# One core, two attention layers: the key-maxima matmuls of the graph layer get a new placement and order on TensorE

## The reference, cut to what matters

```
for c in range(6):                        # nodes; sources are earlier nodes
    q = ew[c, 0] * (nodes[in_q] @ We[eq] + be[eq])
    k = ew[c, 1] * (nodes[in_k] @ We[ek] + be[ek])
    v = ew[c, 2] * (nodes[in_v] @ We[ev] + be[ev])
    o = _mha(q, k, v, Wq[c], Wk[c], Wv[c], Wo[c])     # 8 heads of 16, softmax over 1024 keys
    nodes[c] = act_w[c] * o + q
out = layernorm(nodes[5]) * ln_g + ln_b
```

## Time and profile before

| what | value |
|---|---|
| median of 3 runs | 3166.3 us (3165.73 to 3174.5) |
| the profiled execution's own time | 3165.4 us |
| its span | 3163.4 us |
| PE busy | 2896.4 us, 92% of the span |
| DVE busy | 2419.2 us, 76% |
| ACT busy | 2144.4 us, 68% |
| POOL busy | 380.2 us, 12% |
| mean granted clock of PE | 0.974 |

### The profile page before, as it was taken

The page is one execution under the profiler, slowest core; times in us unless marked ns, Lnnn a source line. Parts: engine busy times, 40 slices in busy tenths (PEclk is TensorE's granted clock), DMA queues, the critical chain, the costliest instruction groups (busy, mean ns, idle before and its releaser), DMA issues. The chain is left out here.

```text
span 3163.4 us, 49154 instructions
## 1 busy us (share of the span) xinstructions
PE 2896.4 (92%) x19007; PEld 1293.5 (41%) x19007; DVE 2419.2 (76%) x3075; ACT 2144.4 (68%) x2683; POOL 380.2 (12%) x322
## 2 busy tenths in 40 slices
PE   5699999999779999999999999999999999999994
PEld 4356656665433333333333333333333333333331
DVE  6655656565868888888888888888888888888843
ACT  1155656555447777777777777777777777777783
POOL 0000000000001111111101111111111110111114
PEclk9699999999979999999999999999999999999996
DMA  6000000004244434435444444443453544345202
GB/s 178 18 11 2 28 2 22 8 23 82 59 94 77 104 93 88 111 93 111 75 100 95 94 104 99 86 97 94 88 110 97 107 74 105 95 88 110 53 22 88
DMA packets 144399, 243.90 MB, mean 77 GB/s; under 512 B 56562, under 2 KB 92934, under 8 KB 140838
## 3 DMA queue, kind: packets, MB, share of 16 engines
q1 hardware_dynamic: 143590, 238.67, 34.0%
q10 hardware_dynamic: 576, 2.10, 0.2%
HBM read 163.82 MB, written 74.10 MB: 75 GB/s over the span
## 5 line engine op out<-in xcount | busy, mean ns | idle before, releaser
L1598 ACT ACTIVATE pt_b<-ps_max 128x1024 f32<-128x1024 f32 x1516 | 1491.7, 1025 | 364.5 <-PE ps_max L1469 360.5
L1623 DVE TENSOR_REDUCE mx_b<-ps_pair 128x2 f32<-128x1024 f32 (+1 forms) x989 | 1193.5, 1207 | 166.9 <-PE ps_pair L1455 158.7
L1504 PE MATMUL ps_ctx<-pt_b,vs 128*32 128x512 f32 x6144 | 820.6, 606 | 3.8 <-ACT c_b L1587 3.5
L1623 DVE TENSOR_REDUCE mx_b<-ps_misc 128x1 f32<-128x512 f32 x989 | 677.7, 685 | 144.0 <-PE ps_misc L1455 125.7
L1469 PE MATMUL ps_max<-qs,ks 50*128 50x512 f32 x3032 | 780.4, 436 | 1.3 <-ACT part L1555 0.9
L1455 PE MATMUL ps_pair<-ks,qs 48*128 48x512 f32 x1955 | 512.3, 458 | 84.8 <-DVE mx_b L1623 84.6
L1469 PEld LDWEIGHTS ps_max<-qs,ks 50*128 50x128 f32 x3032 | 353.2, 186 | 344.0 <-ACT pt_b L1598 254.0
L1455 PE MATMUL ps_misc<-ks,qs 48*128 48x512 f32 x989 | 441.8, 447 | 7.1 <-DVE mx_b L1623 0.3
L960 ACT ACTIVATE pt<-ps_max,cb 128x512 f32<-128x512 f32 x340 | 215.0, 686 | 223.3 <-PE ps_max L801 159.5
L1455 PEld LDWEIGHTS ps_pair<-ks,qs 48*128 48x128 f32 x1955 | 207.4, 184 | 364.8 <-DVE mx_b L1623 332.5
L1455 PEld LDWEIGHTS ps_misc<-ks,qs 48*128 48x128 f32 x989 | 183.2, 185 | 333.4 <-DVE mx_b L1623 260.7
(11 more groups left out here) (194 smaller groups left out, 2257.6 us busy)
## 6 DMA issues: line engine op xcount, KB each, us to landing
partd<-part SPq DMA_DIRECT2D x22, 2048.0 KB, 9.1
qs<-partd SPq DMA_DIRECT2D x288, 128.0 KB, 5.6
ks<-partd SPq DMA_DIRECT2D x288, 128.0 KB, 6.7
xv<-node SPq DMA_DIRECT2D x26, 512.0 KB, 5.5
xf<-node SPq DMA_DIRECT2D x24, 512.0 KB, 4.7
node<-nt_b SPq DMA_DIRECT2D x48, 256.0 KB, 2.1
rec_b<-invd SPq DMA_DIRECT2D x368, 32.0 KB, 1.8
xq<-node SPq DMA_DIRECT2D x22, 512.0 KB, 3.8
```

What stands on the lines that cost most here:

```text
L1504: ins = pe.matmul(psO[SLOT * i:SLOT * i + SLOT, :], vs[u % 2][:, kb, QUAD * (s // HALF_STEPS) + i], pt[:, (QUAD * S + i) % ENTRIES], start ...
L1598: act.activation(pt[:, e:e + 2].rearrange("p k n -> p (k n)"), at[:], ACT.Exp, scale=SCALE_B).then_inc(exp_done, 1)
L1623: nc.vector.tensor_reduce(mx2[:, at:at + n], (psP, psX)[p % 2][:, 0:CHUNK * n].rearrange("p (h n) -> p h n", h=n), AX.X, ALU.max).then_inc ...
```

## The change

Three things are changed, all in `graph`.

1. `pieces_at` no longer deals the pieces out evenly. `stretches(u)` lists the runs of a unit with their free places ("slots") and an estimate of how far PE has come by the end of each (`PE_PARTS`, `PIECE_PARTS`, `CONTEXT_PARTS`). `placed(u)` then gives each run as many of the next pieces as brings the total closest to that share, but only such numbers that the pieces' matmuls in the run come to an even number; it takes no more pieces than the run has slots. They are spread over the run's slots.
2. `in_turn` orders the matmuls of a score pair and of a piece on PE: if the first would lie on the same row half as the last matmul issued in this run, the two are swapped. It is reset at every operation that uses all rows.
3. `score` writes to the half of the bank that belongs to its head, whichever goes first; the second one issued signals. The wait for the rows of maxima stands ahead of the pair.

Nothing is added to or taken from any engine's work: the same 86 pieces, rounds and contexts per unit, the same sizes, buffers and semaphores.

```
+        PE_PARTS = {"score": 3, "turn": 3, "values": 11, "project": 11, "output": 20}
+        PIECE_PARTS, CONTEXT_PARTS = 3, 10
+
+        def stretches(u):
+            out, slots, parts, total = [], [], 0, 0
+            for r, (kind, _, _) in enumerate(ROUND[u]):
+                slots.append((r, 0))
+                if kind != "score":
+                    out.append((slots, total))
+                    slots = []
+                total += PE_PARTS[kind] + PIECE_PARTS * NM // len(ROUND[u])
+                slots.append((r, 1))
+                if steps_at(u, r):
+                    out.append((slots, total))
+                    slots, total = [], total + CONTEXT_PARTS
+            return out + [(slots, total)], total
+
+        def placed(u):
+            at, p = {}, 0
+            runs, total = stretches(u)
+            for slots, end in runs:
+                if not slots:
+                    continue
+                choices = [m for m in range(p, min(p + len(slots), NM) + 1) if sum(SIZES[p:m]) % 2 == 0]
+                m = min(choices, key=lambda m: abs(NM * end - total * m))
+                if slots is runs[-1][0]:
+                    m = NM
+                n = m - p
+                for k in range(n):
+                    i = len(slots) // 2 if n == 1 else k * (len(slots) - 1) // (n - 1)
+                    at.setdefault(slots[i], []).append((u + 1, p + k))
+                p = m
+            return at
+
+        PLACED = [placed(u) for u in range(LAST)]
+
         def pieces_at(u, r, half):
-            if u == LAST:
-                return []
-            todo = [(u + 1, p) for p in range(NM)]
-            k, n = 2 * r + half, 2 * len(ROUND[u])
-            return todo[len(todo) * k // n:len(todo) * (k + 1) // n]
+            return PLACED[u].get((r, half), []) if u < LAST else []
...
+                def in_turn(rows):
+                    order = list(range(len(rows)))
+                    if rows[0] == last_rows[0]:
+                        order.reverse()
+                    last_rows[0] = rows[order[-1]]
+                    return order
...
-                    for k in range(SIZES[p]):
+                    for k in in_turn([(at + k) % 2 for k in range(SIZES[p])]):
...
+                        if kind != "score":
+                            last_rows[0] = None
                         if kind == "score":
-                            score(w, k, to[:, 0:CHUNK])
-                            score(w, k + 1, to[:, CHUNK:TOK]).then_inc(s_ready, 1)
+                            if k % (NS // 2) == 0:
+                                pe.wait_ge(mrow[k // (NS // 2)], MROWS_B * (w + 1))
+                            for e in in_turn((0, 1)):
+                                ins = score(w, k + e, to)
+                            ins.then_inc(s_ready, 1)
...
                         for S in steps_at(u, r):
+                            last_rows[0] = None
                             contexts(S)
```

More of the change, by code:

```diff
@@ L1443, in values @@
                     ins.then_inc(v_ready, 1)
+                last_rows = [None]
+                def in_turn(rows):
[4 more added lines that the diff above has]
+                    return order
                 def maxima(w, p):
@@ L1464, in score @@
                 def score(u, n, to):
-                    if n % (NS // 2) == 0:
-                        pe.wait_ge(mrow[n // (NS // 2)], MROWS_B * (u + 1))
                     h, qc, kb = QUAD * (n // (NS // 2)) + n % QUAD, n // QUAD // KB % NCHUNK, n // QUAD % KB
                     rows = slice(P // 2 * (h % 2), P // 2 * (h % 2) + KROWS_B)
-                    return pe.matmul(to, ks[u % 2][rows, h // 2, P * kb:P * kb + P],
+                    return pe.matmul(to[:, CHUNK * (n % 2):CHUNK * (n % 2) + CHUNK], ks[u % 2][rows, h // 2, P * kb:P * kb + P],
                                      qs[u % 2][rows, h // 2, CHUNK * qc:CHUNK * qc + CHUNK], start=True, stop=True)
```

## The result

The changed kernel takes 3315.4 us in the median of 4 runs (3310.6 to 3321.9) against 3166.0 before: 1.047 times as long, 95% interval 1.044 to 1.050. It is slower, as forecast (3304 us), and inside the range. The profiled execution took 3311.6 us, with a span of 3309.7.

What follows compares the result with a forecast made beforehand. PE sets the pace (busy 89.16 of 93.07 us a unit), partly waiting for buffers DVE must reduce. Steps sum to 99.1 us, +6.0 for 23 units, 138 us on 3165.4, plus 0.9: 3304 us, range 3270 to 3340.

Steps and rivals of the forecast that it cites:

- one pair: Steps with one pair, two score rounds and three waves: 8 per inner unit at 1.90 us, 15.2 in all.
- single, pair, single: Steps whose second single waits for its buffer: 10 per inner unit at 2.70 us, 27.0 in all.
- four pieces: Steps with four pieces in a run, buffers used twice: 4 per inner unit at 3.85 us, 15.4 in all.
- with a projection: Steps with single-pair-single, projection, pair: 4 per inner unit at 4.42 us, 17.7 in all.
- with an output: Two steps per inner unit about an output: 5.3 us with single-pair-single ahead of it, 5.05 with it behind.
- composed steps: The 14 of 32 steps per unit not priced straight from a like step; 0.1 us off each gives 32 us.
- The saved waves: Even runs need 128 waves per inner unit, not 145: 17 saved at 0.235 us, 4.0 us a unit, 92 in all.
- The swap: Putting the half not used last first within a pair was costed at nothing, as the array does it already.
- strict program order: Skill's rule that matmuls start and end in order; by it the change would save 20 waves, 4.7 us per unit.
- The faster one: Second singles start without stall, leaving the saved waves: 3074 us, 4%; by strict order 3058 us, another 1%.
- The slower one: Bursts of pieces pile up on DVE, or the clock stays low longer in unit 0: 3343 to 3382 us, 9%.
- more total wait of PE's weight loads on DVE's reductions: Sign expected in a unit after the change, most of it for singles; before, 14.3 us for pairs and 11.5 for singles.

Runs made afterwards that it cites:

- order-alone run: Kernel before with the new order inside score pairs and pieces but the old placement of the pieces: 3164.7 us, 1.0001 times the kernel before.
- short reductions: DVE's reductions cut to the first 32 of each 512 columns: 3028.4 us in the kernel before, 3050.0 us in the changed kernel.
- The first cut: DVE's reduction of a single reads 256 of its 512 columns: changed kernel 3195.2 us, kernel before 3124.9 us.
- placement-alone run: Changed kernel without the swap, scores and pieces always issued in the old order: 3316.3 us, 1.049 times the kernel before.
- opposite placement: Kernel before with a table placing pieces in units 1 to 21, nearly every run one pair and one single: 3087.3 us, 0.975 times the kernel before.

## Why the prediction was right

**The step prices.** These are contexts-to-contexts times of one inner unit of the changed kernel beside the terms of the sum:

| step | times | forecast | measured |
|---|---|---|---|
| one pair | 8 | 1.90 | 1.89 to 1.90 |
| single, pair, single | 10 | 2.70 | 2.69 to 2.73 |
| four pieces | 4 | 3.85 | 3.83, 3.84, 3.84, 3.94 |
| with a projection | 4 | 4.42 | 4.42 to 4.44 |
| with an output | 2 | 5.3 and 5.05 | 5.27 and 5.04 |
| with values | 2 | 3.2 and 4.0 | 3.16 and 4.00 |
| with a transpose | 2 | 3.1 each | 3.12 and 3.10 |

Their sum was put at 99.1 and is 99.0. The composed steps are as good as those taken straight from a like step.

**Where the other 11 us are.** The forecast charged 6.0 to each of 23 units, 138 us; the spans differ by 146.3. Timeline, first transposes of units 1 and 22, before and after:

```profile
994.06 0.29 PE L1462 MATMUL ps_max<-ident_sb,mx_b 128*32 128x128 f32 x1
...
2950.72 0.28 PE L1462 MATMUL ps_max<-ident_sb,mx_b 128*32 128x128 f32 x1
```

```profile
1000.63 0.28 PE L1506 MATMUL ps_max<-ident_sb,mx_b 128*32 128x128 f32 x1
...
3088.76 0.28 PE L1506 MATMUL ps_max<-ident_sb,mx_b 128*32 128x128 f32 x1
```

The 21 units between them grew from 1956.66 to 2088.13 us, by 131.5. 21 x 5.96 is 125.2; the 6.3 left are covered by three units in which the clock fell (100.64, 103.17 and 100.55 us). Up to the first of these rows the change costs 6.6 us, of which 2.5 lie ahead of unit 0's first transpose. The other 4.1 are in unit 0 itself, where the clock is still rising and which takes 94.8 us in the order-alone run and 97.7 in the kernel before, with the same placement; part of them is scatter. From the second row on it costs 8.3, of which 7.5 are in unit 22 (97.15 against 89.67), to which I had given the same 6.0. There the clock fell twice (at 3124.79 and at 3158.92, to 0.50 for 3.41 us each). One such fall made two other units 1.5 to 1.6 us longer, so by estimate some 3 of the 7.5 are the clock's. The rest of the gap to the median of 3315.4 is that this median lies 3.8 above the profiled execution, with runs from 3310.6 to 3321.9, much wider than the kernel before in most comparisons (3160.7 to 3166.3 over 13 runs).

**The parts.** The saved waves are real, 0.235 each: the step with three waves takes 1.90 where four take 2.13. The swap was costed at nothing and is nothing. The strict program order of the Trainium skill ("TensorE: Matmul & The Clock Gate", Part 3) was put beside the row with the passing matmul and left out of the sum; the starts in the run without the swap and the 0.84 us in the kernel before with short reductions agree with the row. One reading was off: the 20 waves that the change would save by the strict order, 4.7 us a unit, count three that stand in runs which wait for DVE, and those would have saved nothing.

**The rivals.** The faster one (waits vanish) had its threshold at a turn of 1.27 falling under 0.81. The first cut brought the single's turn to about 1.02, the second to 0.77, which is past the threshold, and still the changed kernel stayed above its partner, by 22 us. So the rival had one condition too few. Some runs still wait for a buffer, and where none does, ACT's exponentials hold half of the ten steps with single, pair, single: these ten take 2.20 to 2.41 and not 2.14. The slower one, at 9%, named bursts that pile up and a clock that stays low longer at its rise in unit 0. Neither is seen: the steps behind a burst take their 1.89 to 1.90, and about the start of unit 0 the clock was low for 37.6 us against 51.2 before. What the clock did cost came later, in six short falls that no rival named.

**A sign that I had wrong.** I expected more total wait of PE's weight loads on DVE's reductions. The waits of the unit after the change, as in the earlier trace rows:

```profile
PEld ps_pair L1499 <- DVE mx_b L1671: 12.7, 14, 1.3
...
PEld ps_misc L1499 <- DVE mx_b L1671: 11.7, 22, 0.8
```

That is 24.4 us where it was 25.8. And the fastest kernel has the most on the pairs:

```profile
PEld ps_pair L1462 <- DVE mx_b L1630: 20.2, 26, 1.0
...
PEld ps_misc L1462 <- DVE mx_b L1630: 6.6, 16, 0.8
```

The view counts the idle time of the weight-load engine and names what ended it. At the head of a run nearly all of that time is spent beside the contexts still in the array, whoever is named. Three first weight loads of runs from the timeline of the changed kernel:

```profile
1929.70 0.19 PEld L1499 LDWEIGHTS ps_pair<-ks,qs 48*128 48x128 f32 x2 [0.84 <-DVE mx_b L1671]
...
1970.72 0.18 PEld L1499 LDWEIGHTS ps_misc<-ks,qs 48*128 48x128 f32 x1 [0.84 <-issue]
...
1973.41 0.19 PEld L1511 LDWEIGHTS ps_max<-qs,ks 50*128 50x128 f32 x2 [0.84 <-ACT pt_b L1646]
```

The 0.84 us is the same each time. What a wait costs was seen only in the timeline, in the distance between the matmuls. I had read the steps there, so the price was right, but as a sign to check by, this total was the wrong one.

## What to carry to other kernels

Before matmuls are regrouped to fill the array, compute the turn of each buffer that they write: start of the matmul to start of the reduction, the reduction, and the release, here 0.53 + 0.69 + 0.05 us. Where a group uses one buffer twice in less than that, PE stands still, as here, however idle the reducing engine is on average; an unpaired matmul at 0.12 us (half of a wave) is cheaper than a stall at 0.57. Price the kernel by kinds of steps read from the timeline, each with the runs that it is made of, and count how often each kind occurs after the change; this gave a unit within 0.1%. And before a saved wave is counted as time, look at the next engine in the step: here two exponentials take 2.02 us, so with the reductions out of the way a step of 1.90 only moved the wait into the one behind it.

## What I had not expected of the hardware

**The clock falls though PE is never idle for long.** Between the first and the last unit the kernel before ran at full clock in the profiled execution. The changed one has six short falls there, the longest in its slowest unit (2488.55 to 2591.72, 103.17 us). By stretch, ahead of it, in it and behind it:

```profile
2555.90:2561.70 5.80, 4.37 (x31) 1.56 (x29) 4.21 (x6) 4.34 (x6) 0.45 (x1) 0.99 1.06 130
2561.70:2568.40 6.70, 6.70 (x30) 2.47 (x22) 3.62 (x5) 2.60 (x3) 0.00 (x0) 0.50 0.49 64
2568.40:2574.00 5.60, 5.54 (x40) 1.82 (x38) 4.46 (x5) 4.97 (x7) 1.28 (x1) 1.00 0.05 13
```

The granted clock is 0.50 in the middle row, the lower of the two levels, 1.2 GHz. Ahead of it PE was busy for 4.37 of 5.80 us, behind a transpose and two waits for DVE; its longest idle time there was 0.73 us. Ahead of the six falls PE was busy for 4.37 to 5.09 of 5.80 us, and none of its idle times there was longer than 0.86 us. In the placement-alone run there are falls too. With singles halved, where the stalls are shorter, the changed kernel has none inside the units, and the mean clock of its four runs is 0.975 to 0.977, against 0.968 to 0.973 for the change. But with few stalls a fall can come as well: the opposite placement has one inside units 1 to 22 (at 1084.43), and so has the kernel before with singles halved (at 2821.26). So the clock fell without a long idle time ahead, and oftenest where there were most stalls. That the stalls are the cause was not tested by itself, and why one such stretch is followed by a fall and most of them not stays open.

**The next limits.** With DVE out of the way, two others show. ACT's exponentials hold the score rounds wherever a step is shorter than two of them (0.22 us in the row above). And the second output of a unit waits for POOL and, behind it, for the DMA that spreads the inverse denominators (1.97 us in the row above); behind it the clock fell as well. By estimate from the 87.25 us of those units, whoever wants to go below some 87 us a unit will have to move that chain.
